# Weights split in place, fused products formed inside the first turn, x loaded into a second tile

## The chip, the cores and the metric

The kernel runs on 1 core of one Trainium2 chip. The metric is the device time of one execution in microseconds, here of that core.

## What is computed

x is 128 boards of 64 squares with 256 features. Four layers follow each other, each on h = relu(layernorm(x)) and each added to x: layer 0 is attention with 8 heads and masks per head, layers 1 and 3 are attention with 4 heads masked by adj, and layer 2 is a graph layer with a gate.

```
h = relu(layernorm(x));  x = x + out(softmax(mask(q(h) k(h)^T)) v(h)) + bo     # layers 0, 1, 3
# layer 2, for each of 4 heads:
Wh = h @ W^T + bW;  e = Wh @ attn;  A = tanh(where(adj, e @ Wh^T, 0));  hp = relu(A @ Wh)
ha = cat(hp) @ A_w^T;  hf = h @ fc_w^T
coeff = sigmoid(hf @ g1_w^T + ha @ g2_w^T + gbias);  x = x + hf * coeff + ha * (1 - coeff)
```

All in float32. The kernel writes each weight and each activation as a high part (float32r) and the rest (low part) and makes three products of them. The weights of `e` and `Wh` are multiplied together once, ahead of the work: t1 = attn and W, then g = W and t1 (M_G), and fc with g1 (M_FG + 1).

## The kernel before, in words

Tiling: four boards (256 tokens) make a group, 32 groups in all. Two slots take turns: slot 0 has the even groups and slot 1 the odd ones, so there are 16 turns of two groups. Each slot has its own four banks of PSUM and its own tiles (`X`, `XN`, `HT` and others). The tile `X` holds the running x of the group, `XN` its normed form and, in layer 3 (a == 2), the final sum that is stored.

Steps: `STEPS` is the list of one group's steps (norm_steps, q, k, v, scores, mask, max, exp, soft, pt, heads, pv, out, and those of layer 2). Each of TensorE, ScalarE, VectorE and POOL runs through this list in its own program and does its part of each step. `passes` interleaves the two slots by a table `ORDER`, which was written out by hand: for each engine a lag (with slot 0's first step, slot 1 takes up its previous group so many steps ahead of its end) and for each of slot 0's steps how many steps of slot 1 follow it. A step in which an engine has nothing to do still counts. In the first turn slot 1 has nothing from a turn before, so slot 0 works alone through layers 0 and 1 and into layer 2.

The start (L367 to L541): SP loads the constants, the biases and then eight pieces of weights of 1 MB (`RAWM`), then x, adj and adjT of both slots. ScalarE writes the high parts of the weights (`split_hi`, L769), VectorE the low parts (`split_lo`, L901). TensorE makes t1 (L478), the attn vectors (L485), g (L491), the last product (L500) and the vectors u (L507), and waits for all the splits (L519 to L524) before it begins the first group. `RAWM` shares its memory with the tiles of the turns (Q, K, V and others).

The turns: `norm` (L967) makes `XN` from `X`; for a == 0 it waits that the last store from `XN` is done. "bias" (L1001) adds the output's bias to `X` behind the transposes ("turn"). For the 8 heads of layer 0 TensorE's scores (L590) wait for ScalarE's copy of v, since they write its bank. In SP's `turn` (L392), x of the next group is loaded (L376) once the last residual (`res`, L1057) is written, and then the group is stored (L406). VectorE's order at the change of groups is that bn_stats of the new x stands ahead of the other slot's `rs` (L1075), which TensorE needs for the fourth head of layer 2 (`r_lo`, L656).

## Time and profile before

| | us |
|---|---|
| median of 3 runs | 2044.17 (2043.49 to 2051.04) |
| the profiled execution's own time | 2054.13 |
| its span in the profile | 2052.2 |
| TensorE busy | 1863.7 (91%) |
| VectorE busy | 1401.5 (68%) |
| ScalarE busy | 953.2 (46%) |
| mean granted clock of TensorE | 0.966 of full speed |
| x load, from issue to landing (median of 32) | 2.8 |
| store of a group, from issue to landing (median of 32) | 2.9 |

The page gives each engine's busy time and counts. A timeline gives instructions in order of time, with the idle time ahead of them and what ended it. Windows give the busy time by engine in a stretch, with the granted clock (1.00 is 2.4 GHz, 0.50 is 1.2 GHz). The chain of waits goes back from the last instruction to what released each step. TensorE's matmuls overlap, so their busy time isn't its peak.

### The profile page before, as it was taken

To read this page: it belongs to the slowest core of one execution; us is meant where nothing else is said; L and a number is where in the kernel's file an instruction comes from. 1 tells how busy PE (TensorE), PEld (TensorE's weight loads), DVE (VectorE), ACT (ScalarE), POOL (GpSimd) and SP (SyncE) were. 2 spreads that over 40 slices of the span, in tenths; PEclk is the share of its full clock that TensorE was granted. 3 is DMA by queue.
4 is the path that set the end of the run, shared out by engine and by line. 5 is a ranking of instruction groups with operands and counts; after the bars stand their busy time and mean duration, and the time that the engine had idled before them with its cause. 6 is when DMAs were issued, how large, how long until landed. Compare 5 with 4: busy or idle time off the path is not lost.

```text
span 2052.2 us, 58068 instructions
## 1 busy us (share of the span) xinstructions
PE 1863.7 (91%) x23607; PEld 1632.1 (80%) x23607; DVE 1401.5 (68%) x3776; ACT 953.2 (46%) x3578; POOL 184.6 (9%) x297
## 2 busy tenths in 40 slices
PE   7699999999999999999999999999999999999997
PEld 6588778788778788778788878888878878877876
DVE  4466776767777677676777676777667677677763
ACT  3344544444544544454544554444454454454452
POOL 0000011000011001001001001100001100001100
PEclk8699999999999999999999999999999999999998
DMA  5000000000000000000000000000000000000000
GB/s 190 1 3 13 13 12 12 3 13 13 13 11 13 13 3 13 13 13 11 13 3 13 13 13 11 13 3 13 13 13 11 13 3 13 13 13 11 12 7 6
DMA packets 36532, 30.62 MB, mean 15 GB/s; under 512 B 11568, under 2 KB 36144, under 8 KB 36336
## 3 DMA queue, kind: packets, MB, share of 16 engines
q1 hardware_dynamic: 36336, 27.48, 4.4%
q8 instruction: 187, 3.06, 0.6%
q14 instruction: 9, 0.07, 0.0%
HBM read 19.08 MB, written 8.39 MB: 13 GB/s over the span
## 4 chain that ended last, share of the span: by engine, by line
PE 43%; issue 29%; DVE 12%; ACT 6%; DMA 5%; POOL 4%; SPq 0%; POOLq 0%; DVEq 0%
PE ps L453 38%; DMA x<-x 4%; ACT probs L819 4%; POOL small L432 3%; PE ps L613 2%; DVE small L957 2%; PE ps L539 2%; DVE xn L972 2%; DVE small L963 1%; DVE probs L1047 1%; POOL row_terms L436 1%; ACT probsT L826 1%; DVE f L1117 1%; ACT hT L794 1%; DVE xn L1057 1%
## 5 line engine op out<-in xcount | busy, mean ns | idle before, releaser
L453 PE MATMUL ps<-hT,w_hi 128*128 128x256 f32 x2560 | 501.3, 288 | 9.6 <-ACT hT L794 6.4
L453 PE MATMUL ps<-w_hi,hT 128*128 128x256 f32 (+1 forms) x1536 | 432.4, 346 | 0.0
L453 PEld LDWEIGHTS ps<-hT,w_hi 128*128 128x128 f32 x2560 | 412.4, 191 | 24.7 <-ACT hT L794 11.1
L819 ACT ACTIVATE probs<-probs,small 128x64 f32<-128x64 f32 x1024 | 341.8, 338 | 90.5 <-DVE small L1037 90.2
L453 PE MATMUL ps<-hT,w_lo 128*128 128x256 f32 x1280 | 334.6, 283 | 0.0
L432 POOL TENSOR_TENSOR small<-small,consts 128x1 f32<-128x1 f32 x256 | 149.6, 584 | 1789.6 <-DVE small L965 1789.6
L453 PEld LDWEIGHTS ps<-w_hi,hT 128*128 128x128 f32 x1536 | 268.0, 188 | 44.2 <-DVE wh L1089 10.1
L453 PE MATMUL ps<-w_lo,hT 128*128 128x256 f32 (+1 forms) x768 | 249.7, 337 | 0.0
L453 PEld LDWEIGHTS ps<-hT,w_lo 128*128 128x128 f32 x1280 | 244.4, 191 | 0.0
L794 ACT ACTIVATE hT<-ps 128x256 fp32r<-128x256 f32 x256 | 88.0, 383 | 311.1 <-PE ps L539 311.1
L453 PE MATMUL ps<-w_hi,oT 128*128 128x256 f32 x768 | 194.5, 326 | 23.9 <-DVE oT L888 22.9
L819 ACT ACTIVATION_READ_ACCUMULATOR probs<-probs,small 128x1 f32 x1024 | 194.4, 190 | 0.0
L453 PEld LDWEIGHTS ps<-w_hi,oT 128*128 128x128 f32 x768 | 145.6, 214 | 36.4 <-DVE oT L888 33.9
L957 DVE BATCH_NORM_STATS2 small<-x 128x6 f32<-128x256 f32 x256 | 107.5, 420 | 79.3 <-DMA x<-x 78.2
L453 PEld LDWEIGHTS ps<-w_lo,hT 128*128 128x128 f32 x768 | 144.9, 189 | 8.8
L972 DVE TENSOR_SCALAR xn<-x,small 128x256 f32<-128x256 f32 x256 | 125.0, 502 | 31.5 <-POOL small L432 29.1
L613 PE MATMUL ps<-consts,probs 128*128 128x128 f32 x512 | 99.3, 297 | 43.9 <-DVE probs L1047 43.6
L811 ACT ACTIVATE v<-ps 128x512 f32<-128x512 f32 x96 | 57.2, 596 | 175.9 <-PE ps L453 175.9
L826 ACT ACTIVATE probsT<-ps 128x256 f32<-128x256 f32 (+1 forms) x192 | 86.2, 449 | 103.5 <-PE ps L613 103.2
L539 PE MATMUL ps<-consts,xn 128*128 128x128 f32 x512 | 94.4, 292 | 41.6 <-DVE xn L972 41.6
L453 PE MATMUL ps<-w_hi,ct_hi 128*128 128x256 f32 x512 | 127.1, 286 | 5.1 <-DVE ct_lo L1101 4.8
L453 PE MATMUL ps<-probsT,v 64*64 64x64 f32 (+1 forms) x4096 | 95.7, 234 | 39.0 <-issue 39.0
(114 smaller groups left out, 3325.7 us busy)
## 6 DMA issues: line engine op xcount, KB each, us to landing
raw_mats<-mats SPq DMA_DIRECT2D x8, 1024.0 KB, 10.6
x<-x SPq DMA_DIRECT2D x32, 256.0 KB, 2.8
out<-xn SPq DMA_DIRECT2D x32, 256.0 KB, 2.9
adj<-adjq SPq DMA_DIRECT2D x64, 16.0 KB, 2.1
adjT<-adjt SPq DMA_DIRECT2D x64, 8.0 KB, 2.4
raw_consts<-board_consts SPq DMA_DIRECT2D x1, 451.5 KB, 2.8
w_bias<-rows SPq DMA_DIRECT2D x1, 256.0 KB, 4.5
bias_cols<-cols SPq DMA_DIRECT2D x1, 6.0 KB, 2.6
```

Of the source, the lines that this page charges most:

```text
L432: nc.gpsimd.tensor_tensor(RSTD[s][:, i:i + 1], VE[s][:, i:i + 1], HALF, ALU.pow).then_inc(sm["rstd"], 1)
L436: nc.gpsimd.tensor_tensor(R4[s][:, :, :, :], RS[s][:, :, :].bitcast(F32).unsqueeze(2).broadcast_to([P, TT, H2, SQ]), HEADS.unsqueeze(1).un ...
L453: return nc.tensor.matmul(o, lhsT, rhs, start=start, stop=stop, skip_group_check=True)
L539: last = nc.tensor.transpose(bank(s, H_BANKS[c])[:, t * P:t * P + P], XN[s][:, t * D + c * P:t * D + c * P + P], IDENT)
L613: last = nc.tensor.transpose(bank(s, 1 - i)[:, at:at + P], PR[s][:, j, at:at + P], IDENT)
L794: fn(HT[s][:, 0, c, :], bank(s, H_BANKS[c])[:, 0:TOK], ACT.Relu).then_inc(S[s]["hT_hi"], 1)
L811: fn(V[s][:, :, :], bank(s, 3), ACT.Copy).then_inc(sm["v_sb"], 1)
L819: last = fn(p, p, ACT.Exp, bias=ROWMAX[s][:, row:row + 1], accum_out=ROWSUM[s][:, row:row + 1])
L826: fn(PTS[s][:, j, at], bank(s, 1 - i)[:, at], ACT.Copy).then_inc(sm["pt_sb"], 1)
L957: nc.vector.bn_stats(STATS[s][:, t, :], X[s][:, t * D:t * D + D]).then_inc(S[s]["bn"], 1)
L963: nc.vector.bn_aggr(MV[s][:, t, :], STATS[s][:, t, :]).then_inc(sm["var"], 1)
L972: ts(XN[s][:, t * D:t * D + D], X[s][:, t * D:t * D + D], MV[s][:, t, 0:1], RSTD[s][:, t:t + 1], ALU.subtract, ALU.mult).then_inc(S[s]["xn ...
```

## The change

The raw weights are loaded into the memory that their low parts will hold (`RAWLO` over `WLO`) and, for two operands of the products, their high parts' (`RAWHI` over `WHI`), in the order in which the first group needs them, with x of slot 0 ahead of all. `split_hi`, `split_lo` and the products no longer stand ahead of the first turn; a function `prepare` on TensorE, ScalarE and VectorE runs behind named steps of slot 0 in the first turn and does them there. Two matmuls with the raw Wo become four with its high and low parts.

x is loaded into a second tile, `XP`, behind `ha_ps` of the same slot's group before; bn_stats, norm and bias of layer 0 read it, and bias writes `X`. Layer 3's sum is written to `X` in place and stored from there, and bias of layer 0 waits for the last store.

The step "bias" moves, in all three attention layers, from behind norm_steps to behind the last max. `ORDER` is not changed.

The diff, cut to its core (`prepare` of TensorE, then of ScalarE, then of VectorE):

```diff
-SPLITS = [(M_W, R_WT, 4), (0, 0, 4), (4, 4, 4), (8, 8, 4), (M_A, R_AW, 4), (M_FG, R_FCT, 1), (M_G2, R_G2T, 1)]
+IN_L0, IN_ATT, IN_W, IN_FC, IN_FCN, IN_G, IN_L1, IN_WT, IN_A, IN_L3 = range(10)
+LOADS = {IN_L0: (0, 0, 4), IN_ATT: (M_G, R_ATT, 4), IN_FC: (M_FG, R_FCT, 1), IN_G: (M_FG + 1, R_G1T, 2),
+         IN_L1: (4, 4, 4), IN_WT: (M_W, R_WT, 4), IN_A: (M_A, R_AW, 4), IN_L3: (8, 8, 4)}
+SPLITS = [(IN_L0, 0, 2), (IN_L0, 2, 2), (IN_L1, 4, 4), (IN_WT, M_W, 4), (IN_A, M_A, 4), (IN_FC, M_FG, 1),
+          (IN_G, M_G2, 1), (IN_L3, 8, 4)]
...
                 softmax += [("mask", a, u), ("max", a, u)]
-            softmax += [("exp", a, u) for u in us[:half + 1]] + [("soft", a, u) for u in us[:half]]
+            softmax += [("bias", a, 0)] + [("exp", a, u) for u in us[:half + 1]] + [("soft", a, u) for u in us[:half]]
             softmax += [("pt", a, 0)] + [("exp", a, u) for u in us[half + 1:]] + [("heads", a, 0)]
             softmax += [("soft", a, u) for u in us[half:]] + [("pt", a, 1), ("pv", a, 0), ("heads", a, 1), ("pv", a, 1)]
-            return (norm_steps(a) + [("bias", a, 0)] + [(k, a, i) for k in ("q", "k", "v") for i in range(2)]
+            return (norm_steps(a) + [(k, a, i) for k in ("q", "k", "v") for i in range(2)]
                     + [("scores", a, 0)] + softmax + [("out", a, 0), ("out", a, 1)])
...
                 done = 0
                 for k in range(n):
                     step(0, STEPS[k], now)
+                    if first and prepare is not None:
+                        prepare(*STEPS[k])
                     for done in range(done + 1, done + merge[k] + 1):
...
-                sp.dma_start(RAWM[:, 4 * n:4 * n + 4, :, :],
-                             mats_in[4 * n:4 * n + 4, :, :].rearrange("m (c p) o -> p m c o", p=P)
-                             ).then_inc(raw_sems[max(n - 2, 0)], 16)
             def load_x(s, g):
-                sp.dma_start(X[s][:, :].rearrange("p (t d) -> p t d", t=TT), x_v[:, g, :, :]).then_inc(S[s]["x_in"], 16)
+                sp.dma_start(XP[s][:, :].rearrange("p (t d) -> p t d", t=TT), x_v[:, g, :, :]).then_inc(S[s]["x_in"], 16)
             def load_adj(s, g):
...
+            def load_raw(n):
+                load_mats(n, RAW[n], *LOADS[n][1:])
+            load_x(0, 0)
+            load_raw(IN_L0)
+            load_adj(0, 0)
+            load_raw(IN_L1)
+            load_raw(IN_ATT)
+            load_mats(IN_W, WNAT, R_WNAT, H2)
+            load_mats(IN_FCN, RAWHI[:, M_FG + 1:M_FG + 2, :, :], R_FCNAT, 1)
+            load_raw(IN_G)
+            load_raw(IN_WT)
+            load_raw(IN_A)
+            load_raw(IN_FC)
+            load_raw(IN_L3)
+            load_x(1, 1)
+            load_adj(1, 1)
             for s in range(SLOTS):
-                load_x(s, s)
-                load_adj(s, s)
                 load_adjT(s, s)
             def turn(s, g, gnext, now):
...
                     load_adjT(s, gnext)
-                sp.wait_ge(S[s]["res"], now.six[5])
-                if gnext is not None:
+                    sp.wait_ge(S[s]["ha_ps"], now.two[1])
                     alone(sp)
                     load_x(s, gnext)
-                sp.dma_start(out_v[:, g, :, :], XN[s][:, :].rearrange("p (t d) -> p t d", t=TT)
+                sp.wait_ge(S[s]["res"], now.six[5])
+                sp.dma_start(out_v[:, g, :, :], X[s][:, :].rearrange("p (t d) -> p t d", t=TT)
                              ).then_inc(S[s]["stored"], 16)
...
             last.then_inc(setup["terms_zero"], 1)
-            passes(pool, step, ORDER["pool"])
+            passes(pool, step, None, ORDER["pool"])
...
+            def prepare(k, a, i):
+                if (k, a, i) == ("v", 0, 1):
+                    pe.wait_ge(setup["rows"], 4)
...
+                elif (k, a, i) == ("scores", 0, 0):
+                    pe.wait_ge(setup["bw_sb"], 1)
+                    pe.wait_ge(setup["bv"], 1)
+                    for n in range(3):
+                        o = PS[:, 6 + n // 2, n % 2 * D:n % 2 * D + D]
+                        last = mm(o, SELR[:, 1, :], RAWROWS[:, (n + 1) * D:(n + 1) * D + D], True, n > 0)
+                        if n == 0:
+                            for c in range(DC):
+                                mm(o, BVB[:, c, :], WHI[:, 3, c, :].bitcast(F32), False, False)
+                                mm(o, BVB[:, c, :], WLO[:, 3, c, :].bitcast(F32), False, c == DC - 1)
+                    last.then_inc(setup["bo_ps"], 1)
+                    pe.wait_ge(raw[IN_ATT], 16)
...
+                    last.then_inc(setup["vec_ps"], 1)
+                    pe.wait_ge(raw[IN_W], 16)
+                    for h in range(H2):
+                        if h == 0:
+                            pe.wait_ge(setup["bv"], 1)
+                        elif h == 1:
+                            pe.wait_ge(setup["vec_sb"], 1)
+                        else:
+                            pe.wait_ge(setup["t1_sb"], h - 1)
...
+                        last.then_inc(setup["t1_ps"], 1)
+                elif (k, a, i) in (("out", 0, 1), ("scores", 1, 0)):
+                    first = 2 * a
+                    pe.wait_ge(setup["bo_sb"], 1)
+                    for h in range(first, first + 2):
+                        pe.wait_ge(setup["t1_sb"], max(h + 1, 3 + h % 2))
+                        if h >= 2:
+                            pe.wait_ge(setup["g_lo"], h - 1)
+                        at = 0
+                        for ic in range(DC):
+                            for c in range(DC):
+                                at = ic * H2 + h
+                                mm(PS[:, 6, at:at + 1], T1[:, h, c, ic * P:ic * P + P], bcol[:, h, c:c + 1],
+                                   c == 0, c == DC - 1)
+                                mm(PS[:, 7, at:at + 1], WNAT[:, h, c, ic * P:ic * P + P], A1[:, c, h:h + 1],
+                                   c == 0, c == DC - 1)
+                        for ic in range(DC):
+                            for c in range(DC):
+                                last = mm(PS[:, 5 - h % 2, ic * D:ic * D + D], WNAT[:, h, c, ic * P:ic * P + P],
+                                          T1[:, h, c, :], c == 0, c == DC - 1)
+                        last.then_inc(setup["g_ps"], 1)
+                    if a == 1:
...
+                elif (k, a, i) == ("out", 1, 1):
+                    pe.wait_ge(raw[IN_FCN], 16)
+                    pe.wait_ge(raw[IN_G], 16)
...
+                elif (k, a, i) == ("turn", L2, 1):
...
+                elif (k, a, i) == ("turn", 0, 1):
+                    pe.wait_ge(setup["w_lo"], 1)
+                elif (k, a, i) == ("k", 0, 1):
+                    pe.wait_ge(setup["w_lo"], 2)
+                elif (k, a, i) == ("turn", 1, 1):
+                    pe.wait_ge(setup["w_lo"], 3)
+                elif (k, a, i) == ("turn", 2, 1):
+                    pe.wait_ge(setup["w_lo"], 8)
...
+            def split_hi(n):
+                load, m, k = SPLITS[n]
+                act.wait_ge(raw[load], 16)
+                fn(WHI[:, m:m + k, :, :], RAWLO[:, m:m + k, :, :], ACT.Copy).then_inc(setup["w_hi"], 1)
+            def t1_out(h):
...
+            split_hi(0)
+            split_hi(1)
+            def prepare(k, a, i):
+                if (k, a, i) == ("turn", 0, 1):
+                    split_hi(2)
+                elif (k, a, i) == ("v", 0, 1):
...
+                elif (k, a) == ("exp", 0) and i[0] in (1, 2):
+                    t1_out(2 * i[0] - 2)
+                    t1_out(2 * i[0] - 1)
+                elif (k, a, i) == ("out", 0, 1):
+                    g_hi(0)
+                    g_hi(1)
+                elif (k, a, i) == ("turn", 1, 1):
+                    split_hi(3)
+                elif (k, a, i) == ("q", 1, 1):
+                    split_hi(4)
+                elif (k, a, i) == ("v", 1, 1):
+                    split_hi(5)
+                    split_hi(6)
+                elif (k, a) == ("exp", 1) and i == units(1)[1]:
+                    g_hi(2)
+                    g_hi(3)
+                elif (k, a, i) == ("out", 1, 1):
+                    g_hi(4)
+                elif (k, a, i) == ("e", L2, 3):
+                    split_hi(7)
...
+            def prepare(k, a, i):
+                if (k, a, i) == ("norm", 0, 1):
+                    split_lo(0)
+                    split_lo(1)
+                elif (k, a, i) == ("turn", 0, 1):
+                    bias_rows()
+                elif (k, a, i) == ("k", 0, 1):
+                    split_lo(2)
+                elif (k, a, i) == ("v", 0, 1):
+                    dve.wait_ge(setup["bv_ps"], 1)
...
+                elif (k, a) == ("max", 0) and i[0] == 1:
+                    dve.wait_ge(setup["vec_ps"], 1)
+                    nc.vector.tensor_copy(A1[:, :, :], PS[:, 4, 0:DC * H2]).then_inc(setup["vec_sb"], 1)
+                elif (k, a) == ("max", 0) and i[0] == 3:
+                    dve.wait_ge(setup["bo_sb"], 1)
+                elif (k, a, i) == ("norm", 1, 1):
+                    g_lo(0)
+                    g_lo(1)
+                elif (k, a, i) == ("turn", 1, 1):
+                    split_lo(3)
+                elif (k, a, i) == ("k", 1, 1):
+                    split_lo(4)
+                elif (k, a, i) == ("v", 1, 1):
+                    split_lo(5)
+                    split_lo(6)
+                elif (k, a) == ("soft", 1) and i == units(1)[0]:
+                    row_vectors()
+                    g_lo(2)
+                    g_lo(3)
+                elif (k, a, i) == ("norm", L2, 1):
+                    g_lo(4)
+                elif (k, a, i) == ("e", L2, 3):
+                    split_lo(7)
...
                 x_ready(s, a, t, v)
-                nc.vector.bn_stats(STATS[s][:, t, :], X[s][:, t * D:t * D + D]).then_inc(S[s]["bn"], 1)
+                nc.vector.bn_stats(STATS[s][:, t, :], (XP if a == 0 else X)[s][:, t * D:t * D + D]).then_inc(S[s]["bn"], 1)
             def stats(s, a, t, v):
...
-            def norm(s, a, t, v, before):
-                if a == 0 and t == 0 and before is not None:
-                    dve.wait_ge(S[s]["stored"], before)
+            def norm(s, a, t, v):
                 dve.wait_ge(S[s]["rstd"], norm_halves(a, v)[t])
-                ts(XN[s][:, t * D:t * D + D], X[s][:, t * D:t * D + D], MV[s][:, t, 0:1],
+                ts(XN[s][:, t * D:t * D + D], (XP if a == 0 else X)[s][:, t * D:t * D + D], MV[s][:, t, 0:1],
                    RSTD[s][:, t:t + 1], ALU.subtract, ALU.mult).then_inc(S[s]["xn_ready"], 1)
             def masks(s, v):
...
-                    x = X[s][:, :].rearrange("p (t d) -> p t d", t=TT)
+                    x, old = (y[s][:, :].rearrange("p (t d) -> p t d", t=TT) for y in (X, XP if a == 0 else X))
                     dve.wait_ge(sm["xn_ready"], norm_halves(a, v)[1])
-                    tt(x, x, BOB[:, a:a + 1, :].broadcast_to([P, TT, D]), ALU.add).then_inc(sm["x_bias"], 1)
+                    if a == 0 and v.before is not None:
+                        dve.wait_ge(sm["stored"], v.before)
+                    tt(x, old, BOB[:, a:a + 1, :].broadcast_to([P, TT, D]), ALU.add).then_inc(sm["x_bias"], 1)
                 elif k == "masks":
                     masks(s, v)
...
                     at = slice(i * D, i * D + D)
                     dve.wait_ge(sm["x_bias"], n)
                     dve.wait_ge(sm["y_ps"], v.six[2 * a + i])
-                    tt((XN if a == 2 else X)[s][:, at], bank(s, Y_BANKS[i])[:, 0:D], X[s][:, at], ALU.add
+                    tt(X[s][:, at], bank(s, Y_BANKS[i])[:, 0:D], X[s][:, at], ALU.add
                        ).then_inc(sm["res"], 1)
```

## Rows read from the trace of the kernel before

**Rows 1.** The page: busy time, share of the span and instructions.
```profile
PE 1863.7 (91%) x23607; PEld 1632.1 (80%) x23607; DVE 1401.5 (68%) x3776; ACT 953.2 (46%) x3578; POOL 184.6 (9%) x297
```
**Rows 2.** Windows: stretch, length, busy by engine, clock, DMA share, GB/s.
```profile
26.00:34.00 8.00, 8.00 (x31) 6.90 (x32) 7.11 (x6) 5.05 (x4) 0.00 (x0) 0.57 0.41 127
34.00:44.00 10.00, 10.00 (x67) 9.30 (x65) 4.92 (x6) 5.22 (x7) 0.00 (x0) 1.00 0.00 0
54.00:101.00 47.00, 29.86 (x315) 23.92 (x313) 21.01 (x60) 16.34 (x69) 2.50 (x5) 0.65 0.00 1
```
**Rows 3.** Timeline of SyncE: start, duration, operation; slot 0's loads and first store.
```profile
164.25 0.40 SPq L376 DMA_DIRECT2D x<-x  x1
164.83 0.41 SPq L406 DMA_DIRECT2D out<-xn  x1
...
1875.22 0.38 SPq L376 DMA_DIRECT2D x<-x  x1
```
**Rows 4.** Timeline, 405 to 420 us: behind the x load at 410.41.
```profile
413.27 0.43 DVE L957 BATCH_NORM_STATS2 small<-x 128x6 f32<-128x256 f32 x1 [2.10 <-DMA x<-x]
...
417.15 0.76 PE L539 MATMUL ps<-consts,xn 128*128 128x128 f32 x4 [0.30 <-DVE xn L972]
```
**Rows 5.** Waits: who waited for what, us in total, times, longest.
```profile
DVE small L957 <- DMA x<-x: 78.2, 30, 4.1
```
**Rows 6.** Windows behind the x loads: the second, and the sum of all 30.
```profile
227.95:233.65 5.70, 4.38 (x33) 3.75 (x31) 3.54 (x10) 0.00 (x0) 2.24 (x3) 1.00 0.11 39
...
sum 171.00, PE 154.81 PEld 138.19 DVE 130.65 ACT 26.82 POOL 65.86; mean PE 5.16 PEld 4.61 DVE 4.35 ACT 0.89 POOL 2.20
```
**Rows 7.** Timeline, slot 1's layer 0: the copy of v, the scores.
```profile
362.24 0.60 ACT L811 ACTIVATE v<-ps 128x512 f32<-128x512 f32 x1 [2.00 <-PE ps L453]
...
363.53 0.91 PE L453 MATMUL ps<-kT,qT 32*64 32x64 f32 x64
```
**Rows 8.** Timeline, 386 to 410 us: K copy of slot 1, transposes of slot 0.
```profile
391.64 0.68 DVE L1017 COPY kT<-ps 128x512 f32<-128x512 f32 x1
...
392.70 0.76 PE L539 MATMUL ps<-consts,xn 128*128 128x128 f32 x4 [0.80 <-DVE xn L972]
```
**Rows 9.** Timeline, 322 to 360 us: slot 0's layer 1 beside slot 1.
```profile
331.31 0.76 DVE L986 SCALAR_TENSOR_TENSOR hT<-ps,hT 128x256 fp32r<-128x256 f32 x2
...
340.82 0.47 PE L613 MATMUL ps<-consts,probs 128*128 128x128 f32 x2 [0.50 <-DVE probs L1047]
```
**Rows 10.** Timeline of the start: a split, a copy of t1, one-column matmuls, bn_stats.
```profile
16.05 2.29 DVE L888 TENSOR_TENSOR w_lo<-raw_mats,w_hi 128x2048 fp32r<-128x2048 f32 x1 [3.96 <-ACT w_hi L772]
...
22.74 0.60 ACT L779 ACTIVATE raw_mats<-ps 128x512 f32<-128x512 f32 x1 [1.13 <-PE ps L453]
...
40.40 0.36 PE L453 MATMUL ps<-xn,raw_mats 128*128 128x1 f32 x2
...
40.63 0.36 PE L453 MATMUL ps<-bias_cols,raw_mats 128*128 128x1 f32 x2
...
51.57 0.43 DVE L957 BATCH_NORM_STATS2 small<-x 128x6 f32<-128x256 f32 x1
```
**Rows 11.** The chain of waits: start, duration, what; the start and the first turn.
```profile
3.53 10.73 DMA raw_mats<-mats
...
66.56 1.27 PE ps L613 x4
...
75.73 0.42 DVE x L1057
...
79.09 0.49 PE ps L539
...
87.41 0.44 DVE probs L1031
...
91.91 0.58 PE ps L613 x2
```
**Rows 12.** Windows: a stretch behind a wait of TensorE.
```profile
404.00:407.00 3.00, 2.59 (x27) 2.06 (x25) 1.69 (x6) 0.37 (x2) 0.00 (x0) 0.68 0.00 0
```

More of the change, by code:

```diff
@@ L328, in build, with passes @@
         STEPS = att_steps(0) + att_steps(1) + L2_STEPS + att_steps(2)
[L330 removed]
+        def passes(eng, step, prepare, order, unrolled=False):
             n = len(STEPS)
@@ L763, in _ @@
             fn(RAWRH[:, :], RAWR[:, :], ACT.Copy).then_inc(setup["rows"], 1)
-            act.wait_ge(setup["bw_ps"], 1)
-            for n in range(2):
-                last = fn(BWB[:, n * 512:n * 512 + 512], PS[:, 6 + n, :], ACT.Copy)
-            last.then_inc(setup["bw_sb"], 1)
-            def split_hi(first, last):
-                for m, r, k in SPLITS[first:last]:
-                    act.wait_ge(raw_sems[max(r // 4 - 2, 0)], 48 if r < R_WNAT else 16)
-                    fn(WHI[:, m:m + k, :, :], RAWM[:, r:r + k, :, :], ACT.Copy).then_inc(setup["w_hi"], 1)
@@ L898, in _ @@
-            dve.wait_ge(setup["rows"], 4)
-            nc.vector.tensor_copy(ROWS[:, :], RAWROWS[:, 0:D].bitcast(F32)).then_inc(setup["rows"], 1)
-            def split_lo(first, last):
-                for n in range(first, last):
-                    m, r, k = SPLITS[n]
-                    dve.wait_ge(setup["w_hi"], n + 1)
-                    lo_part(WLO[:, m:m + k, :, :], RAWM[:, r:r + k, :, :], WHI[:, m:m + k, :, :]
-                            ).then_inc(setup["w_lo"], 1)
-            split_lo(0, 1)
@@ L918, in _, with split_lo, g_lo @@
-            split_lo(3, 4)
-            for n in range(H2 + 1):
+            dve.wait_ge(setup["consts"], 2)
+            def split_lo(n):
+                _, m, k = SPLITS[n]
+                dve.wait_ge(setup["w_hi"], n + 1)
+                lo_part(WLO[:, m:m + k, :, :], RAWLO[:, m:m + k, :, :], WHI[:, m:m + k, :, :]
+                        ).then_inc(setup["w_lo"], 1)
+            def g_lo(n):
                 dve.wait_ge(setup["g_hi"], n + 1)
-                m, b = (M_G + n, n) if n < H2 else (M_FG + 1, 5)
+                m, b = (M_G + n, 5 - n % 2) if n < H2 else (M_FG + 1, 5)
```

224 lines of the change are left out of this document (98 added, 126 removed).

## The prediction

> **What bounds the kernel now.** I read the page first. TensorE is busy for 1863.7 us, 91% of the span, against 68% of VectorE [rows 1]. So only two things can be won: the start, and the idle time that TensorE has left in the turns. The windows of the start say what the first is made of: in 54 to 101 us, when slot 0 works alone, TensorE is busy 29.9 of 47 us at a clock of 0.65 [rows 2]: a chain of dependent steps, not a bound engine. In the turns I read SyncE's timeline: slot 0's loads of x are issued at 164.25 and, 14 turns on, at 1875.22 us, so a turn of both slots takes 122.2 us [rows 3].
>
> **The next x in a second tile.** Today x is loaded once its slot's last residual is written, and VectorE stands 2.10 us at bn_stats for it; TensorE then waits 0.30 us for xn at the transposes [rows 4]. All 30 waits of VectorE make 78.2 us [rows 5]. VectorE is not the bound, so TensorE's idle time behind it counts: at the transposes, and at the fourth head's e, which wants the row term rs that VectorE makes behind bn_stats. In thirty windows of 5.7 us, each from 2.3 us after an x load, TensorE is busy 154.81 of 171.0 us [rows 6]. Their 16.2 us of idle time is what the prefetch can give back. The upper end is 24 us: were every pair of windows like its worst (0.3 and 1.3 us idle), 15 pairs would make that. The lower end is 4, if rs stays late for its other input. I take 16, the sum measured. The new load follows ha_ps, over 20 us before x is used, for a landing of 2.8 us: hidden. On SP it stands ahead of the wait for the residual; only the store is queued behind it. The wait for the store moves from norm to bias, which comes behind the scores, long after the 2.9 us landing: 0, and if that cover went, 2.9 us a turn and slot.
>
> The Trainium skill (Trainium Kernel Development and Optimization, section Best Practices) says to double-buffer so that DMA and compute overlap. Read as "the whole wait comes back", it would give 78 us where the windows of TensorE give 16; that is rival 4.
>
> **The bias step moved, the table of turns unchanged.** The table counts steps. With "bias" moved from behind the transposes to behind the last max, every step in between is one place earlier in the count, and meets the other slot's steps elsewhere. I wrote out the order of each engine from the table, before and after. Four places matter, each once a turn.
> (a) Slot 1, layer 0. TensorE's scores come directly behind v, no longer behind two wh steps of slot 0. They wait for ScalarE's copy of v, for the banks. Today that copy starts at 362.24 and takes 0.60 us, hidden behind the wh matmuls; scores start at 363.53 [rows 7]. Without that cover TensorE stands from about 362.1 to 362.9: 0.8 us (0.6 to 0.9).
> (b) Slot 1, layer 1, beside slot 0's layer 2. VectorE's K copy of 0.67 us, which today fills the time in which POOL makes rstd (391.64, ahead of the xn for which TensorE waits until 392.70), goes ahead of the stats [rows 8]. The xn is then 0.5 us later; scores of slot 1 fill part of that gap. 0.4 us (0 to 0.7).
> (c) Slot 0, layer 1. A mask of 0.41 us goes ahead of slot 1's hT_lo, which today starts at 331.31, as soon as hT_hi is there [rows 9]. 0.3 us (0 to 0.4).
> (d) Behind it the bias of 0.68 us now precedes slot 1's soft, for whose probs TensorE waited 0.50 us until 340.82 [rows 9]. 0.3 us (0 to 0.6).
> In layer 0 the bias itself is covered, since exp of the second unit stands in ScalarE behind the other slot's tanh; and one wh copy comes 0.3 us earlier. Together 0.8 + 0.4 + 0.3 + 0.3 - 0.3 = 1.5 us in 15 turns: 22. Bounds: 15 x 0.3 = 5 (only half of (a) lasts, the rest is taken from later waits) and 15 x 2 = 30. I take 18, since TensorE's later waits absorb some.
>
> **The start.** Slot 0's first bn_stats starts at 51.57 us today [rows 10]. A megabyte of weights takes about 2.7 us (the third lands 10.73 us after its issue at 3.53, all behind the constants) [rows 11]. With x (256 KB) and layer 0's weights ahead, x is there near 7 and those weights near 9.5; bn_stats can start at 7.6, as soon as the constants are copied. That is a lead of 44 us. From there the added work takes some of it back, in order:
> VectorE, layer 0: split_lo of two halves 2.3 us, masks 0.7, hT_lo 0.8, bias_rows 3.7, K 0.9, split_lo of layer 1 2.29, BVB 0.4, from ScalarE's w_hi at 10.6: 22 us. TensorE's bo matmuls wait for it.
> TensorE, layer 0, ahead of the first transposes of probs: bo 4 us, the attn vectors 5.5, t1 of four heads. One head is 1.13 + 0.60 = 1.73 us by the rhythm of its copies at full clock [rows 10], so 7 us, or 14 at half; taken 9.5. The transposes come near 41 us instead of 66.56 [rows 11]. Lead 25.
> TensorE, behind out of layer 0: u and g of two heads. A one-column f32 matmul takes 0.23 us at full clock (40.40 to 40.63) [rows 10]; eight of them and g make 3.5 us a head, so 7 for two, 14 at half; taken 11.5. The residual's chain from 75.73 to 79.09 covers 3.3 of that [rows 11]. Lead 17, and 16 behind ScalarE's g_hi.
> Layer 1: the same 11.5 us stand between scores and probs, and before soft of the second unit VectorE also does row_vectors and two g_lo, 2.7 us. Today this stretch, from the first mask at 87.41 to the last transposes at 91.91, takes 4.5 us [rows 11]; so some 10 are lost. Lead 6. The last product and the split of layer 3 cost 1 to 2 us more.
> Result: 4 us won. The end points: all that TensorE work at full clock, 18 won; all at half, 10 lost. The set-up has run at both levels: 1.00 in 34 to 44 us, 0.57 in 26 to 34 [rows 2], the second behind one-column matmuls.
>
> **Sum.** -16 (x) + 18 (order) - 4 (start) = -2 us. On the profiled execution's own 2054.1 us that is 2052; the median of the timed runs is 10 us lower, so 2044.2 - 2 = 2042. The clock in the turns is a further spread: it falls for a few microseconds where TensorE has waited (0.68 in 404 to 407 us) [rows 12]. A few more or fewer such falls are up to 8 us either way.
>
> **Rivals.**
> 1. The order costs little (8 us) and the start goes at full clock, with 14 us won: -16 + 8 - 14 = -22, so 2022. For it: every second window behind x has over 0.5 us of idle time, and slot 0 alone leaves TensorE idle for 17 us. Against: place (a) has no cover that I can find. 0.29.
> 2. The other side: the changed order sets the turns. Places (a) to (d) in full make 2 us a turn, 30 in all, and the start wins nothing: -16 + 30 = +14, so 2058. It decides as soon as a turn gains over 1.7 us of TensorE idle time at those places. For it: each of the four has a row with little or no slack. Against: TensorE's later waits, of 0.5 us and more, can take up a delay. 0.23.
> 3. The prefetch does not do what it says: x is early, but TensorE meets the same waits, because rs still hangs on ScalarE's r_hi. Then x gives 4 us: 2054. Against: TensorE waits longest for xn there, not for rs [rows 4]. 0.04.
> 4. All of VectorE's wait returns, as every step of both slots hangs on it: 78 instead of 16, so 1980. Against: TensorE is 91% busy in those very windows [rows 6]. 0.01.
> 5. The forecast, 2034 to 2054: 0.43.
>
> **Chances.** 0.5% is 10 us, about what a measurement of this kernel can tell from no change. Faster by more: rivals 1 and 4 and the forecast's edge, 0.32; same 0.43; slower 0.25, rivals 2 and half of 3. The range joins rivals 1 and 2 with some of the clock's spread: 2019 to 2065.
>
> **What would show it.** bn_stats of x no longer waits for a DMA, and TensorE's 16 us of idle time behind it is gone. In slot 1's layer 0 a TensorE wait of some 0.8 us for the copy of v stands ahead of scores. The distance of one slot's store issues, 122.2 us today, stays within 0.5. The first store, issued at 164.83 us today [rows 3], is issued 2 to 8 us earlier. The prediction is wrong if a turn changes by over 1 us, if that first store moves by over 12 us, or if the share of half clock in the turns changes much.

## The result, and the profile after

The changed kernel takes 2055.64 us (median of 20 runs) where the kernel before took 2046.99 us on the same chip: ratio 1.0037, interval 1.0022 to 1.0052. On a second chip it took 2051.32 us where the kernel before took 2048.83: 1.0019 (0.9993 to 1.0045). The forecast was 2 us less than before, 2042. The time lies inside the stated range of 2019 to 2065 and within 0.5% of the kernel before, but it moved the other way. The two profiled executions differ less than the medians: 2053.41 us with a span of 2051.1 after, 2054.13 with 2052.2 before.

The page after, its line of busy times, to be set beside [rows 1]. No engine does much more or less.

```profile
PE 1859.1 (91%) x23611; PEld 1636.8 (80%) x23611; DVE 1401.1 (68%) x3777; ACT 961.0 (47%) x3579; POOL 186.0 (9%) x297
```

SyncE's timeline after, to be set beside [rows 3], where slot 0's first store was issued at 164.83 us; the one 14 turns on was issued at 1875.79.

```profile
142.98 0.42 SPq L438 DMA_DIRECT2D out<-x  x1
...
175.64 0.40 SPq L390 DMA_DIRECT2D x_next<-x  x1
205.93 0.40 SPq L438 DMA_DIRECT2D out<-x  x1
...
1873.35 0.40 SPq L438 DMA_DIRECT2D out<-x  x1
```

So the start gained 21.9 us. Fourteen turns took 123.60 us each, not 122.21, and lost 19.4 of it; what follows them took another 1.3.

The start after, timeline, to be set beside [rows 10] and [rows 11].

```profile
8.13 0.43 DVE L1070 BATCH_NORM_STATS2 small<-x_next 128x6 f32<-128x256 f32 x1 [8.13 <-DMA x_next<-x]
...
25.69 3.63 PE L484 MATMUL ps<-bias_cols,raw_lo 128*128 128x1 f32 x32
29.18 8.84 PE L484 MATMUL ps<-raw_hi,raw_lo 128*128 128x256 f32 x32
37.86 0.60 PE L670 MATMUL ps<-consts,probs 128*128 128x128 f32 x4
...
45.76 0.42 PE L484 MATMUL ps<-bias_cols,t 128*128 128x1 f32 x2
...
53.09 0.60 PE L596 MATMUL ps<-consts,xn 128*128 128x128 f32 x4
...
70.58 0.69 PE L670 MATMUL ps<-consts,probs 128*128 128x128 f32 x2 [1.87 <-DVE probs L1159]
```

And a row of its chain of waits (start, duration): layer 0's weights landed at 11.25 us, for 9.5 forecast.

```profile
2.90 8.35 DMA raw_lo<-mats
```

u and g of two heads stand between 45.76 and 53.09: 7.3 us, where 11.5 had been taken. Layer 1's last transposes of probs start at 70.58, not at 91.91. The lead over the kernel before is 28.7 us at the first transposes of probs (66.56 to 37.86), 26.0 at layer 1's transposes (79.09 to 53.09), 21.3 there and 21.9 at the first store.

TensorE's waits in one turn after (timeline, idle time and what ended it in brackets). The first four lie 51 to 58 us behind slot 0's store, the others in slot 1's layer 0 and at the change to slot 0's layer 3.

```profile
194.00 0.46 PE L484 MATMUL ps<-probsT,v 64*64 64x64 f32 x16 [0.52 <-issue]
195.20 0.39 PE L484 MATMUL ps<-w_hi,oT 128*128 128x256 f32 x1 [0.73 <-DVE oT L969]
196.95 0.69 PE L670 MATMUL ps<-consts,probs 128*128 128x128 f32 x2 [0.77 <-DVE probs L1159]
200.69 0.70 PE L484 MATMUL ps<-probsT,v 64*64 64x64 f32 x16 [0.52 <-issue]
...
213.63 0.39 PE L484 MATMUL ps<-hT,w_hi 128*128 128x256 f32 x1 [0.36 <-ACT hT L875]
219.80 0.90 PE L484 MATMUL ps<-kT,qT 32*64 32x64 f32 x64 [0.78 <-ACT v L892]
...
249.51 0.44 PE L596 MATMUL ps<-consts,xn 128*128 128x128 f32 x2 [0.21 <-DVE xn L1082]
250.36 0.44 PE L596 MATMUL ps<-consts,xn 128*128 128x128 f32 x2 [0.42 <-DVE xn L1082]
251.16 0.38 PE L484 MATMUL ps<-hT,w_hi 128*128 128x256 f32 x1 [0.36 <-ACT hT L875]
```

Waits of TensorE (PE) and of its weight loads (PEld) over the 14 turns (us in total, times, longest): before, then after.

```profile
PEld ps L539 <- DVE xn L972: 42.1, 65, 1.0
PE ps L539 <- DVE xn L972: 28.4, 56, 0.8
PEld ps L613 <- DVE probs L1047: 33.2, 28, 1.7
PE ps L613 <- DVE probs L1047: 29.4, 29, 1.5
PEld ps L453 <- DVE rs L1075: 6.2, 15, 1.2
PE ps L453 <- DVE rs L1075: 2.7, 4, 1.0
PE ps L453 <- ACT hT L794: 10.2, 28, 0.4
```

```profile
PEld ps L596 <- DVE xn L1082: 23.1, 48, 0.7
PE ps L596 <- DVE xn L1082: 13.6, 42, 0.4
PEld ps L484 <- ACT hT L875: 33.7, 56, 0.6
PE ps L484 <- ACT hT L875: 20.4, 56, 0.4
PE ps L484 <- ACT v L892: 10.9, 14, 0.8
```

The waits for rs are gone and those for xn are about half; a new one for v has come, and those for hT have doubled. The remaining wait of VectorE for x is the first load's:

```profile
DVE small L1070 <- DMA x_next<-x: 8.1, 1, 8.1
```

One more thing differs. From the records of the granted clock, TensorE spent 65 us of the 14 turns at 1.2 GHz before, and 99 us after; in the start it was 58 us before and 17 after. Within the timed runs of each kernel the time rises by 0.17 to 0.38 us for each us at half clock (half clock of a run = 2 x (1 - mean clock) x span), for most by about 0.33. This is a slope between runs, so what follows from it is an estimate. I use 0.33 below to compare turns at equal clock: turn - 0.33 x (half clock in the turns) / 14.

### The profile page after: what moved, and what is told of

It reads as the page before. It is cut to its first block, busy times and chain, and to the rows that moved or that the text cites. A ratio compares the mean times of both kernels' runs of the same rounds, so it can differ in the third digit from the quotient of the medians.

```text
span 2051.1 us, 58084 instructions
## 1 busy us (share of the span) xinstructions
PE 1859.1 (91%) x23611; PEld 1636.8 (80%) x23611; DVE 1401.1 (68%) x3777; ACT 961.0 (47%) x3579; POOL 186.0 (9%) x297
## 4 chain that ended last, share of the span: by engine, by line
PE 52%; issue 30%; DVE 7%; ACT 7%; POOL 3%; DMA 0%; POOLq 0%; DVEq 0%; SPq 0%
PE ps L484 47%; ACT probs L900 3%; POOL small L464 3%; PE ps L670 2%; PE ps L596 2%; DVE small L1070 2%; ACT hT L875 1%; DVE small L1076 1%; DVE xn L1082 1%; DVE probs L1159 1%; POOL row_terms L468 1%; ACT probsT L907 1%; DVE x L1169 1%; ACT oT L910 0%; ACT v L892 0%
## 5 line engine op out<-in xcount | busy, mean ns | idle before, releaser
L484 PE MATMUL ps<-w_hi,hT 128*128 128x256 f32 (+1 forms) x1536 | 427.5, 344 | 0.0
L484 PE MATMUL ps<-w_hi,oT 128*128 128x256 f32 x768 | 199.5, 332 | 19.5 <-DVE oT L969 18.8
L484 PEld LDWEIGHTS ps<-w_hi,oT 128*128 128x128 f32 x768 | 150.3, 221 | 30.8 <-DVE oT L969 28.8
L1096 DVE SCALAR_TENSOR_TENSOR hT<-ps,hT 128x256 fp32r<-128x256 f32 x256 | 98.7, 417 | 69.4 <-ACT hT L875 69.4
L484 PEld LDWEIGHTS ps<-probsT,v 64*64 64x64 f32 (+1 forms) x4096 | 68.6, 127 | 79.1 <-issue 69.2
L484 PE MATMUL ps<-w_lo,ct_hi 128*128 128x256 f32 x512 | 125.1, 283 | 0.0
```

The lines of the kernel that those rows point to most:

```text
L484: return nc.tensor.matmul(o, lhsT, rhs, start=start, stop=stop, skip_group_check=True)
L1096: stt(HT[s][:, 1, c, :], bank(s, H_BANKS[c])[:, 0:TOK], 0.0, HT[s][:, 0, c, :].bitcast(F32), ALU.max, ALU.subtract).then_inc(S[s]["hT_lo"], 1)
```

## The experiments

All kernels, each as its ratio to the kernel before on the same chip. Turn and half clock (us at 1.2 GHz) are those of the one profiled execution; the us column is the median of the timed runs.

| kernel | us | ratio (interval) | turn | at 1.2 GHz in 14 turns | turn at equal clock |
|---|---|---|---|---|---|
| before | 2047 to 2051 | 1 | 122.21 | 65 | 120.7 |
| changed | 2055.64 | 1.0037 (1.0022-1.0052) | 123.60 | 99 | 121.3 |
| e11 changed, again | 2051.32 | 1.0019 (0.9993-1.0045) | 123.68 | 116 | 120.9 |
| e4 prefetch only | 2010.23 | 0.9811 (0.9786-0.9836) | 119.45 | 41 | 118.5 |
| e3 bias step moved only | 2083.59 | 1.0153 (1.0125-1.0181) | 124.31 | 41 | 123.3 |
| e9 start only | 2035.24 | 0.9933 (0.9909-0.9957) | 121.94 | 48 | 120.8 |
| e15 order and prefetch | 2072.57 | 1.0109 (1.0092-1.0126) | 123.62 | 116 | 120.9 |
| e16 order and start | 2066.71 | 1.0084 (1.0057-1.0112) | 124.33 | 41 | 123.4 |
| e10 layer 0's bias late | 2061.29 | 1.0060 (1.0038-1.0082) | 122.81 | 44 | 121.8 |
| e7 two places of layer 0 | 2062.43 | 1.0070 (1.0045-1.0095) | 123.09 | 31 | 122.4 |
| e1 changed, table aligned | 2018.30 | 0.9843 (0.9819-0.9867) | 121.22 | 37 | 120.3 |
| e2 as e1, bias early in 1, 3 | 2010.72 | 0.9799 (0.9774-0.9824) | 120.20 | 27 | 119.6 |
| e8 as e1, bias early in turns | 1996.33 | 0.9748 (0.9724-0.9771) | 119.48 | 44 | 118.4 |
| e12 TensorE's order aligned | 2046.20 | 0.9992 (0.9974-1.0010) | 122.91 | 61 | 121.5 |
| e13 attention places aligned | 2053.12 | 1.0014 (0.9993-1.0034) | 123.56 | 99 | 121.2 |
| e14 layer 0 places aligned | 2035.79 | 0.9947 (0.9924-0.9970) | 122.22 | 92 | 120.0 |

### One part alone

e3: the kernel before with the step moved. VectorE's addition moves with it, and the table joins other steps.

```diff
-            softmax += [("exp", a, u) for u in us[:half + 1]] + ...
+            softmax += [("bias", a, 0)] + [("exp", a, u) for u in us[:half + 1]] + ...
-            return (norm_steps(a) + [("bias", a, 0)] + ...
+            return (norm_steps(a) + ...
```

> The kernel before with nothing changed but the place of the step bias in the list; the table stays. Theory (the changed order of the two slots costs the turns): the ledger of TensorE's idle time puts +0.78 us a turn at the scores of slot 1's layer 0 (copy of v), +0.36 at q behind its transposes, +0.2 each at two places of layer 1, so 1.5 us a turn, and the clock falls for longer behind them; a turn takes 123.7 to 124.6 us instead of 122.2, the whole 22 to 36 us more than before (ratio 1.011 to 1.018). Rival (the turns got slower through the new x tile or the first turn's leftovers, not through the order): a turn stays within 0.5 us of 122.2, ratio 1.000 to 1.004.

Measured: +31 us, a turn of 124.31, both as expected. The reason was only half right: the clock did not fall for longer (41 us at 1.2 GHz in the turns, against 65), and at equal clock a turn is 2.6 us longer, not 1.5.

e4: the kernel before with only the second tile.

```diff
+                    sp.wait_ge(S[s]["ha_ps"], now.two[1])
                     alone(sp)
                     load_x(s, gnext)          # into XP; bn, norm and bias of layer 0 read it
+                sp.wait_ge(S[s]["res"], now.six[5])
+                sp.dma_start(out_v[:, g, :, :], X[s]...)
```

> The kernel before with the second tile for x alone (the first turn reads x from the old tile). Theory: TensorE's 1.07 us of idle time a turn behind xn and rs goes and nothing takes its place, since a wh step still stands between the transposes and q: a turn takes 121.1 us, the whole is 16 us less (ratio 0.992; 0.989 to 0.994). Rival A (a new wait for hT_hi of 0.36 us takes the place of the old one even with the old order): 11 us less, ratio 0.995. Rival B (x was hidden anyway, other waits take the time back): ratio 0.998 to 1.001. Rival C (all of VectorE's 78 us come back): ratio 0.962.

Measured: -39 us, more than twice what was expected, and outside all three rivals. Waits in its 14 turns:

```profile
PEld ps L541 <- DVE xn L974: 23.7, 39, 1.0
PE ps L541 <- DVE xn L974: 15.8, 28, 0.8
```

Against before, the waits for xn and rs lose 12.6 + 2.7 = 15.3 us in the PE rows and 18.4 + 6.2 = 24.6 us in those of the weight loads. The 14 turns of the profiled execution got 14 x 2.76 = 39 us shorter, 31 of it at equal clock and 8 by 24 us less at half clock. The weight loads' rows are nearer to 31 than the PE rows, though 6 us are in neither.

### The table aligned again

e1 keeps the changed kernel, but an empty step stands where "bias" was, the step behind the last max is gone, and VectorE adds at the exp of the first unit. In e2 and e8 the step at the old place is "bias" again, and they differ in when VectorE adds. The diff is cut to these lines.

```diff
+            return (norm_steps(a) + [("none", a, 0)] + ...                        # e1
-                elif k == "bias":
+                elif k == "exp" and i == units(a)[0]:                             # e1
+                elif (k == "exp" and i == units(0)[0]) if a == 0 else k == "bias":  # e2
+                elif k == ("exp" if a == 0 and v.before is None else "bias") and i in (0, units(a)[0]):  # e8
```

> The changed kernel with an empty step where bias stood, so that the table meets the same steps as in the kernel before; VectorE adds the bias behind the last max, as in the changed kernel. Theory: the start's 22 us stay, the prefetch gives its 16, and what the order cost goes: a turn takes 121.1 to 121.6 us, the whole is 30 to 38 us less than before (ratio 0.981 to 0.985). Rival (the late bias on VectorE is what costs, not the shifted table): a turn takes 122.5 us or more, ratio 0.990 to 0.995.

> As the one before, but in layers 1 and 3 the bias is also added where it was, behind the transposes; only layer 0 adds it late. Theory: the late bias delays soft of slot 1's layer 3 by 0.2 to 0.3 us a turn; this kernel is 0 to 5 us faster than the aligned kernel with the late bias (ratio to before 0.979 to 0.984). Rival (late bias is the cost): 10 us or more faster than the aligned kernel with the late bias.

Measured: against the changed kernel, e1 takes 1.8 to 1.9% less, 36 to 40 us. Against the kernel before it takes 32 us less, as expected, but not for the reasons expected: the prefetch was worth more than 16 us, and the late bias costs something too (e2, e10). e2 was another 8 us faster, between the 0 to 5 expected and the rival's 10, and this with a start at half clock in its profiled execution: its first store came at 155.43 us, that of e1 at 142.58. At equal clock its turn is 0.8 us shorter, the price of the late bias in layers 1 and 3.

> The changed kernel with two parts of its order taken back: the step 'bias' again stands behind the norm steps in the list of steps, with VectorE adding the bias there in layers 1 and 3 and, from the second turn on, in layer 0 too (late in layer 0 only in the first turn, where the bias rows aren't ready). The second x tile and the start inside the first turn stay. The table of turns so joins the same steps of both slots as before. Theory (prefetch -30 us at equal clock, start -10 to -20 by its clock, late bias of layer 0 +1.1 us a turn and gone here): a turn of 119.4 us, 0.5 to 1 less than in the variant whose layer 0 was still late (120.2), first store at 143 to 156 us, 1990 to 2003 us, ratio 0.973 to 0.978. Rival (layer 0's late bias is covered, as the prediction had it): turn 120.2, the same time as that variant, ratio 0.980. It would also be the fastest version.

Measured: 1996.33 us, as expected, 52 us less than the kernel before on the same chip, and the fastest. e2 to e8 is 1.1 us a turn at equal clock: layer 0's late bias, against the rival that it is covered.

### The late bias of layer 0 by itself

e10, the kernel before with one line changed:

```diff
-                elif k == "bias":
+                elif k == ("exp" if a == 0 else "bias") and i in (0, units(a)[0]):
```

> The kernel before with one edit: in layer 0 VectorE adds the output's bias at the exp of the first unit of heads, not behind the transposes. The list of steps and the table are as before, x is loaded as before. Theory: TensorE's first transposes of probs in layer 0 wait longer for VectorE (0.37 us for slot 0, 0.65 for slot 1 by the gaps seen in the variants), 0.75 to 1.1 us a turn: +11 to +16 us, ratio 1.005 to 1.008. The prediction's step (layer 0's late bias is covered): ratio 1.000.

Measured: +12 us, as expected. Its waits in the 14 turns, and the loads of weights that wait in slot 1's layer 0 (timeline); the same loads in the kernel before have no wait.

```profile
PEld ps L613 <- DVE probs L1047: 47.5, 70, 1.7
PE ps L613 <- DVE probs L1047: 28.5, 28, 1.5
```

```profile
370.47 0.20 PEld L613 LDWEIGHTS ps<-consts,probs 128*128 128x128 f32 x2 [0.30 <-DVE probs L1047]
371.02 0.20 PEld L613 LDWEIGHTS ps<-consts,probs 128*128 128x128 f32 x2 [0.35 <-DVE probs L1047]
```

PE's sum doesn't move (29.4 to 28.5), that of the weight loads rises by 14.3, and the turns at equal clock by 14 x 1.1 = 15. So here waits of 0.3 us at the weight loads cost about their full time and leave no idle time in the PE rows, where the matmul before them still shows as busy. The Trainium skill (Perfetto Trace Analysis, section Tensor Engine Instruction) says of this engine that the end time in the profile is an estimate, not a measurement; the trace agrees, with these 14 us.

### The places in layer 0 by themselves

e7 is the kernel before with two entries of TensorE's row changed, a 3 to 4 and a 7 to 6:

```diff
-... 7, 0, 0, 0, 0, 3, 6, 0, 7, 0, 2, 3 ...
+... 7, 0, 0, 0, 0, 4, 6, 0, 6, 0, 2, 3 ...
```

> The kernel before with two entries of TensorE's row of the table changed and nothing else: slot 0's step that stood between slot 1's copy of v and its first scores, and the one between slot 1's transposes of layer 0 and its q, move to where the changed kernel has them. Theory: TensorE then waits 0.78 us a turn for ScalarE's copy of v and 0.36 for VectorE's hT, 1.14 in the trace's idle time and 0.17 more for each wait that the modelled ends hide: 1.1 to 1.5 us a turn, +17 to +23 us, ratio 1.008 to 1.011. Rival (later waits absorb it, at least half): +0 to +9 us, ratio under 1.0045.

Measured: +14 us, between the theory and its rival. The wait for v is there 14 times, as in the changed kernel. The time at half clock in the turns fell by 34 us, and that hid part of the cost: at equal clock a turn is 1.7 us longer.

```profile
PE ps L448 <- ACT v L806: 10.9, 14, 0.8
```

### The start by itself

e9 is e8 with x loaded behind the residual again.

```diff
-                    sp.wait_ge(S[s]["ha_ps"], now.two[1])
+                sp.wait_ge(S[s]["res"], now.six[5])
+                if gnext is not None:
                     alone(sp)
                     load_x(s, gnext)
```

> As the run before, but x of the next group is again loaded behind the last residual (still into its own tile, the store behind it), so only the start differs in order from the kernel before. Theory: turns as in the kernel before at equal clock (120.7 us plus a third of the half clock's time), the x waits of TensorE back (0.3 for xn at the two changes of a turn, 0.6 and 0.8 behind), first store 9 to 22 us earlier by the start's clock: 2025 to 2042 us, ratio 0.989 to 0.996. Against the run before it gives the price of the x load alone with the start changed: 2.1 us a turn, about 32 us. Rival (prefetch worth 16 us): 14 to 18 us between the two runs. Rival (the start wins nothing, as its lead is spent inside the first turn): ratio 1.000.

Measured: -14 us (9 to 19), and 39 us between e9 and e8, where 32 were expected: the load of x again. The start's clock differs between the profiled executions of kernels that share this start. Windows 46 to 62 us (stretch, length, busy by engine, clock), e2 and then the changed kernel:

```profile
46.00:62.00 16.00, 15.65 (x58) 13.73 (x58) 4.54 (x13) 2.54 (x5) 1.19 (x2) 0.50 0.00 1
```

```profile
46.00:62.00 16.00, 15.33 (x137) 14.07 (x137) 10.27 (x18) 7.58 (x10) 1.20 (x2) 0.99 0.01 2
```

Both begin with u and g of two heads there: these take until 59.77 us in e2 and until 53.09 in the changed kernel. Up to 43 us TensorE's rows of the two have the same durations, 0.8 us apart in time. At 0.50 the first store came at 155.43 us, at 0.99 at 142.98. The other kernels with this start had it at 139.63 to 150.74. Whether one kernel's start can run at either level isn't shown, since each was profiled once.

### The sum, and what it lacked

The parts add up to -39 + 31 - 14 = -22 us. The changed kernel is at +4 to +8. It was run again (e11), and three variants took back parts of TensorE's order.

> The changed kernel itself, beside the variants of its table on the same chip. Theory (what the single parts cost and bring doesn't add up to its time: order and late bias +31, prefetch -39, start -14 make -22, and it is +8, since TensorE's clock falls in 10 of 14 turns at 51 to 58 us behind slot 0's store): ratio 1.002 to 1.006 again, 85 to 110 us at half clock in its 14 turns, most of the falls at that place. Rival (the profile was one chance alignment): a ratio near 0.99 here, or falls at other places.

> The changed kernel with one edit: TensorE's row of the table is written so that its instructions join as in the kernel before, in all places. VectorE, ScalarE and POOL keep the shifted rows, and the bias is late. Theory (TensorE's order is what costs: 1.14 us of waits a turn at the two places in layer 0, and the clock's falls with the other two): 2018 to 2030 us, ratio 0.984 to 0.990, turn 121.2 to 121.9, half clock in the turns 35 to 60 us. Rival (VectorE's and ScalarE's shifted orders cost as much): 2035 to 2045, ratio over 0.992.

> The changed kernel with one edit to TensorE's row of the table: only where slot 1's k, v and scores of layer 3 stand between slot 0's probs transposes and heads of layer 1, its order is that of the kernel before. Theory (these orders make the clock fall at 51 to 58 us of the turn): half clock in the turns down from 99 to 40 to 60 us, the waits of 0.78 and 0.36 us at the places in layer 0 stay; 2030 to 2042 us, ratio 0.990 to 0.997. Rival (the clock's falls don't hang on that place's order, but on all that the turn holds): half clock and time within 5 us of the changed kernel, ratio 1.002 to 1.006, or falls elsewhere.

> The changed kernel with one edit to TensorE's row of the table: only the two places of slot 1's layer 0 are as in the kernel before (q of layer 0 behind one step of the other slot, scores behind three steps of it). Theory: the waits of 0.78 us for ScalarE's copy of v and 0.36 us for VectorE's hT go, 1.1 to 1.5 us a turn, so 16 to 21 us less than the changed kernel with the clock as it is: 2030 to 2040, ratio 0.990 to 0.995. Rival (later waits take it up): within 8 us of the changed kernel, ratio over 0.998.

e11 has no edit. Of its 14 turns nine have a fall of the clock there; in the first profile it was eight, not the ten that the expectation says. The edit of the others is TensorE's row of the table alone, written so that slot 1's steps join as before: in e12 everywhere, in e13 only where they meet slot 0's layer 1, in e14 only in slot 1's layer 0. For e14, as the order of TensorE's steps (slot 0's wh and s2, all others slot 1's):

```diff
-wh0 turn0 turn1 [q0] wh1 q1 k0 k1 v0 v1 [scores] wh2 wh3 s2
+wh0 turn0 turn1 wh1 [q0] q1 k0 k1 v0 v1 wh2 wh3 [scores] s2
```

e14 won 15.5 us against e11, as expected. e13 won nothing: its rival held, and the clock still fell at the same place, 53 to 54 us behind slot 0's store, in 12 of 14 turns. e12 was 5 us better than e11, within what the intervals leave open, and far short of e1: its rival held, and my expectation was wrong. What e12 lacks against e1, 28 to 31 us, is the shifted rows of VectorE, ScalarE and POOL, which no run separates. e12's clock did recover for the most part (61 us at 1.2 GHz in the turns, against 116), but at equal clock its turn is 121.5 us, against 120.0 in e14. So aligning TensorE's other places too, with VectorE shifted, was worse than leaving them (e12 against e14: 10 us).

e15 is the kernel before with the edits of e3 and of e4, e16 the changed kernel with the edit of e9.

> The kernel before with two of the three parts: the step 'bias' moved (late bias and shifted table) and x loaded into a second tile behind ha_ps; the start is as before. If the parts simply add, +31 - 39 = -8 us, ratio 0.996, with 40 to 60 us of half clock in the turns. If this pair is what makes the clock fall (fewer waits behind x, more at 51 to 58 us of the turn), the half clock in the turns is 90 us or more and the time +5 to +15 us, ratio 1.003 to 1.007, and the interaction is settled.

> The changed kernel with x of the next group loaded behind the last residual again, so the moved bias step with the changed start and no prefetch. If the parts simply add, +31 - 14 = +17 us, ratio 1.008, half clock in the turns 40 to 60 us. If this pair makes the clock fall, 90 us or more of half clock there and +30 to +40 us, ratio 1.015 to 1.020.

e16 is +17 us (12 to 23), and 31 - 14 = 17: these two add. e15 is +22, neither -8 nor the +5 to +15 of its other case: beside the moved step the prefetch is worth 9 us and not 39. The pair lacks 30 us, which is what the sum lacked (-22 + 30 = +8). Two windows of twelve us, 50 us behind slot 0's stores, of e3 and then of e15 (stretch, length, busy by engine, clock):

```profile
592.03:604.03 12.00, 9.04 (x144) 7.37 (x143) 9.18 (x28) 7.00 (x31) 1.19 (x2) 1.00 0.00 1
...
1710.82:1722.82 12.00, 9.03 (x142) 7.15 (x141) 9.22 (x28) 6.97 (x29) 1.19 (x2) 1.00 0.01 1
```

```profile
588.42:600.42 12.00, 9.46 (x131) 7.82 (x130) 8.25 (x26) 5.75 (x25) 1.20 (x2) 0.71 0.00 1
...
1701.01:1713.01 12.00, 10.10 (x72) 9.01 (x73) 8.17 (x25) 6.20 (x27) 1.20 (x2) 0.57 0.01 1
```

e3 is at full clock in all 14 such windows, e15 below it in 9, and the changed kernel in 8. The prefetch alone brings falls there too: the kernel before is below full clock in 2 of these windows, e4 in 6:

```profile
209.69:221.69 12.00, 9.53 (x122) 7.66 (x120) 8.72 (x27) 7.18 (x30) 1.20 (x2) 0.86 0.01 2
329.14:341.14 12.00, 9.80 (x119) 8.36 (x109) 8.64 (x27) 6.72 (x29) 1.19 (x2) 0.72 0.00 1
```

With the moved step beside it the falls there last longer. Summed over the 14 windows they are 10 us at 1.2 GHz in the kernel before, 27 in e4, 65 in e15 and 47 in the changed kernel, where two of them are:

```profile
192.98:204.98 12.00, 9.46 (x93) 7.95 (x83) 8.77 (x26) 6.09 (x26) 1.19 (x2) 0.65 0.01 2
...
934.57:946.57 12.00, 9.77 (x84) 8.57 (x85) 8.60 (x27) 6.19 (x27) 1.19 (x2) 0.61 0.01 1
```

The waits there have the same lengths in e3, e15 and the changed kernel (0.52, 0.74, 0.77 and 0.52 us), and up to the fall so have those of the weight loads (0.73, 0.88 and 0.97 us). The same transposes in e3 and then in e15: the wait is equal, and the two matmuls that follow it take 0.44 us in one and 0.69 in the other.

```profile
598.45 0.44 PE L613 MATMUL ps<-consts,probs 128*128 128x128 f32 x2 [0.76 <-DVE probs L1047]
```

```profile
593.97 0.69 PE L615 MATMUL ps<-consts,probs 128*128 128x128 f32 x2 [0.76 <-DVE probs L1051]
```

The prefetch does remove its waits in e15 too: 2.4 us a turn at equal clock, against 2.2 alone. At equal clock the turns of the changed kernel add up as well: 120.7 + 2.6 (e3) - 2.2 (e4) + 0.1 (e9) = 121.2 us, for 120.9 and 121.3 measured. The clock takes it back: 116 instead of 41 us at 1.2 GHz in the turns, and by the mean clock of the timed runs 182 instead of 107 us over the whole, so by the slope between runs 75 x 0.33 = 25 of the 30 us. The other 5 are not accounted for.

What stays open is why the clock falls there. In the one profile of each kernel, falls at that place stand in more turns with the prefetch than without it (6 in e4 for 2 before, 9 in e15 for none in e3, 8 in the changed kernel for 1 in e16, 6 in e8 for 1 in e9), and they are longest with the moved step beside it. With the whole table aligned the turns are back at 27 to 44 us of half clock (e1, e2, e8), with 1, 3 and 6 such falls. Neither e13's order nor e14's alone removes them, e12's shortens them to 3.4 us each, and up to the fall TensorE's waits within that stretch don't differ from e3's.

## Why the prediction was wrong

The number was near by luck: all three terms of the sum were off, partly against each other, and a fourth, the clock, stood at nothing. The step that turned the sign is that last one: -2 was forecast, the three parts measured alone make -22, and 30 us that appear only for the moved step and the prefetch together, 25 of them by the clock, make +4 to +8.

**x, -16.** The mechanism was right: VectorE's wait for x is gone, TensorE's waits behind it shrink, and the load is hidden. The size was wrong: -39 us alone (e4, and e9 against e8), outside my 4 to 24. The step that failed is the measure, "TensorE's idle time" from busy time of the windows [rows 6]: PE's ends are modelled, and waits are shown too short there: 15.3 us went in PE's rows and 31 in the turns at equal clock. The other 8 us of the 39 are less time at half clock, for which the sum had no term. Rival 4 (all 78 us) stays wrong; half of it returned. The Trainium skill (Trainium Kernel Development and Optimization, section Best Practices) asks for this double buffer, and the measurement agrees with the rule: 39 us here when it came alone, and 9 beside the moved step (e15 against e3).

**The order, +18.** Measured as e3: +31, at my upper bound of 30; at equal clock 2.6 us a turn, not 1.5. The two parts of it that ran alone, e7 and e10, make 14 + 12 = 26 of the 31. Place (a) came as forecast: 0.78 us, 14 times in 14 turns, for 0.8. A place was missed: one wh step no longer stands between slot 1's transposes and its q in layer 0, and TensorE waits 0.36 us for hT. Both together are e7's +14. Of (b), hT's 0.36 us and less for xn came, 0.2 net in PE's rows; (c) and (d) raised the wait for probs from 0.50 [rows 9] to 0.77 us. The step "in layer 0 the bias itself is covered" failed: it costs 12 us (e10). "TensorE's later waits absorb some" was not borne out: e7's turn grew by 1.7 us at equal clock where its new waits in PE's rows sum to 1.14.

**The start, -4.** Measured as e9: -14 us. The chain of steps was right (bn_stats at 8.13 for 7.6, transposes at 37.86 for 41), and what was mis-sized is the work that takes the lead back. The leads of 25, 17 and 6 us were 28.7, 26.0 and 21.3. The added matmuls of TensorE were taken between the two clocks and ran mostly at the full one (7.3 us for u and g, not 11.5), where my own end point said -18; and in layer 1 some 5 us were lost, not 10. e2 shows that the other level happens. The timed runs of e9 lie 8 to 22 us under the kernel before, so the forecast's 4 was too small at either end.

**The clock, up to 8 us.** This was the largest miss. I took the falls as a spread of either sign, worth nothing in the sum. By e15 they came with the change, and the estimate of their cost is 25 us, three times the spread.

**The rivals.** Rival 1's number, -22, is what the parts measured alone add up to, though with other terms. Rival 2's mechanism, the order in full with a turn 1.7 us or more longer, is e3; in the changed kernel the turn grew by 1.4. The numbers nearest to 2056 are 2054 of rival 3 and 2058 of rival 2, both by luck: rival 3 had TensorE's wait for rs stay, and it went; rival 2 had the start win nothing, and it won 21.9 us in the profile. None of the rivals held a term for the clock, and that decided the sign. The prediction was to be wrong if a turn changes by over 1 us, the first store by over 12 or the half clock much. All three happened: 1.4 us, 21.9 us, and 99 us for 65.

## What to carry to other kernels

A table that counts steps is part of the code: whoever moves a step leaves an empty one in its place, or writes the rows of all engines again, together. That one empty step was worth 36 to 40 us here; TensorE's row written again alone was worth 5. Read the waits of the weight loads beside those of the matmuls, and sum those. And where parts each measured alone don't add up, compare the clock before looking for a further wait: with the old order of steps and an early bias in the turns, the second x tile and the new start give 1996 us (e8).

## What the runs showed of the hardware

In the stretch 50 to 62 us behind slot 0's store, waits of the same lengths at the same steps of TensorE went with a clock of 1.00 in one kernel (e3) and 0.57 to 0.86 in another (e15); no wait of its weight loads in these turns was over 1.9 us in the changed kernel, and the clock fell all the same. Whole kernels that execute the same matmuls so differ by 75 us at half clock, some 25 us of time.

The start with the same steps of slot 0 ran at 0.50 in one kernel (e2) and at 0.99 in another (the changed one) in 46 to 62 us, with 12 us between the first stores.

At heads of bursts of 64-wide matmuls TensorE stands 0.52 us with nothing in the profile that ends it ("issue"), in every kernel here. Why is not shown.
